# The first stage of a two-layer transformer kernel: smaller loads, another order on VectorE, later pair work and unread products on TensorE

## The reference, cut to what matters

```python
x = L0_attn_x                                   # (32, 256, 128) f32: 8192 tokens of 128
xn = _layernorm(x)
x = x + _L0_attn_ref(xn, ...) + _L0_ffn_ref(xn, ...)
# inside: gate logits = gelu(xn @ Wg1.T + bg1) ..., router = relu(xf @ Wr1 + br1) @ Wr2 + br2
xn = _layernorm(x)
x = x + _L1_attn_ref(xn, ...) + _L1_ffn_ref(xn, ...)
# _L1_attn_ref convolves with a kernel that depends on parameters alone:
#   K[h, l] = 2 Re sum_n Ct[h, n] exp(dtA[h, n] * l),  l = 0 .. 255
```

## Time and profile before

| | us |
|---|---|
| median of three runs | 1342.68 |
| profiled execution, own time | 1341.5 |
| its span | 1339.7 |
| PE's last work of the first stage ends | 91.86 |
| first load of the second stage issued by SP | 95.74 |
| first product of the second stage | 100.54 |

### The profile page before, as it was taken

How to read it: one execution, slowest core, us unless ns; L and a number is a source line. 1 busy time by engine, 2 the same in 40 slices (tenths; PEclk the granted TensorE clock), 3 DMA queues, 4 the chain that set the end, 5 groups by cost and what they waited for, 6 DMA issues and landing times. The chain is left out here.

```text
span 1339.7 us, 27122 instructions
## 1 busy us (share of the span) xinstructions
PE 1158.9 (87%) x9434; PEld 830.3 (62%) x9434; DVE 891.8 (67%) x2733; ACT 674.5 (50%) x1087; POOL 746.3 (56%) x908
## 2 busy tenths in 40 slices
PE   0771699999999997999999988999589899888884
PEld 0550355555555545899999885777456676666663
DVE  7917788888888864666666653888664588843321
ACT  1751377777777773444444333555333355533330
POOL 2300688888888862555555451333348377427776
PEclk9985699999999998999999998999699999989997
DMA  9350300000000001222222212224149022334443
GB/s 323 126 182 19 153 26 26 26 26 26 26 26 26 26 30 39 70 72 70 67 72 70 64 55 69 63 64 121 58 153 291 25 61 64 131 122 65 63 64 30
DMA packets 89568, 103.51 MB, mean 77 GB/s; under 512 B 12860, under 2 KB 75004, under 8 KB 89340
## 3 DMA queue, kind: packets, MB, share of 16 engines
q1 hardware_dynamic: 68768, 74.61, 17.6%
q0 software_dynamic: 19968, 26.63, 8.5%
q10 hardware_dynamic: 732, 0.94, 0.2%
HBM read 55.52 MB, written 46.63 MB: 76 GB/s over the span
## 5 line engine op out<-in xcount | busy, mean ns | idle before, releaser
L842 ACT ACTIVATE probs<-ps 128x1024 f32<-128x1024 f32 x256 | 255.0, 1025 | 76.5 <-PE ps L752 76.5
L1160 POOL DMA_INDIRECT y<-slot_y,where x144 | 150.9, 1048 | 144.8 <-DVE slot_y L1141 121.3
L1050 POOL DMA_INDIRECT slots<-rowbuf,slots x192 | 194.8, 1014 | 65.8 <-issue 42.8
L1221 ACT ACTIVATE slot_h<-ps,own 128x256 f32<-128x256 f32 x288 | 120.3, 470 | 153.2 <-PE ps L1192 151.5
L1192 PE MATMUL ps<-slot_x,own 128*128 128x256 f32 x576 | 140.8, 388 | 3.4 <-DVE slot_x L1130 3.1
L1204 PEld LDWEIGHTS ps<-own,slot_h 128*128 128x128 f32 x1152 | 140.0, 192 | 4.2 <-ACT slot_h L1221 0.6
L1204 PE MATMUL ps<-own,slot_h 128*128 128x128 f32 x1152 | 140.3, 276 | 0.2 <-ACT slot_h L1221 0.2
L768 PE MATMUL ps<-probs,vext 128*32 128x256 f32 x2048 | 136.9, 385 | 0.0
L1628 POOL DMA_INDIRECT out<-xT,where x64 | 99.1, 1548 | 40.6 <-DVE xT L1931 25.4
L1192 PEld LDWEIGHTS ps<-slot_x,own 128*128 128x128 f32 x576 | 105.5, 193 | 19.2 <-DVE slot_x L1130 7.5
L1779 ACT ACTIVATE h<-ps,packs 128x512 f32<-128x512 f32 x64 | 44.0, 687 | 91.2 <-PE ps L1680 89.4
(11 more groups left out here) (302 smaller groups left out, 2365.1 us busy)
## 6 DMA issues: line engine op xcount, KB each, us to landing
toeplitz<-conv_kernel SPq DMA_DIRECT2D x16, 1024.0 KB, 7.4
slots<-blank SPq DMA_DIRECT2D x26, 528.0 KB, 7.0
slot_rows<-slots SPq DMA_DIRECT2D x72, 132.0 KB, 2.2
routed<-y SPq DMA_DIRECT2D x32, 256.0 KB, 3.1
packs<-in_experts SPq DMA_DIRECT2D x1, 4624.0 KB, 14.8
packs<-in_experts SPq DMA_DIRECT2D x8, 578.0 KB, 7.2
xT<-slots SPq DMA_DIRECT2D x16, 264.0 KB, 2.7
out<-stream SPq DMA_DIRECT2D x16, 256.0 KB, 2.3
```

Source lines behind the costliest of these rows:

```text
L842: act.activation(probs[:, p % 4, :, :, :].rearrange("p j k t -> p j (k t)"), ps[:, 2 * (p % 2):2 * (p % 2) + 2, :], ACT.Exp, scale=DK ** - ...
L1050: return pool.indirect_dma_start(m["slot_dram"][layer], bass.IndirectOffsetOnAxis(ap=where, axis=0), m["rowbuf"][:, tile, :], None)
L1160: pool.indirect_dma_start(m["y_dram"][layer], bass.IndirectOffsetOnAxis(ap=where[:, j, h:h + 1], axis=0), y[:, j, h, :], None).then_inc(se ...
L1221: ins = act.activation(hidden[:, j % 2, k, :], ps[:, 2 * (j % 2) + k // 2, (k % 2) * LOT:(k % 2) * LOT + LOT], act_func, bias=own[:, j, P_ ...
```

## The change

It sets `LOADS` to 8 (8 tiles, 0.5 MB, a load) and `FIRST` to 6, orders DVE's list so that each doubling follows a measure and a normalise, and adds unread products of constants on PE: eight when the constants have landed, and four ahead of `turn(g)` for g = 1 to 5. They write bank 7, which holds nothing yet.

```diff
--- before.py
+++ after.py
@@ -204,8 +204,9 @@
     QUADS = L2 // 4
     ROUNDS = 4
     PRODUCT_BANK = (7, 5, 6, 7)
-    LOADS = 4
-    FIRST = 4
+    LOADS = 8
+    FIRST = 6
+    WARM_FIRST, WARM_EACH = 8, 4
     with ExitStack() as ctx:
         def sb(name, shape, dt=F32):
             return ctx.enter_context(nc.sbuf_tensor(name, shape, dt))
@@ -454,17 +455,13 @@
             coefficients()
             measure(0)
             begin_powers()
-            measure(1)
-            normalise(0)
-            for i in range(3):
-                double(i)
-            measure(2)
-            normalise(1)
-            double(3)
-            dve.engine_nop().then_inc(sem["pair"], 1)
-            for g in range(3, GROUPS):
+            for g in range(1, GROUPS):
                 measure(g)
                 normalise(g - 1)
+                if g <= ROUNDS:
+                    double(g - 1)
+                if g == ROUNDS:
+                    dve.engine_nop().then_inc(sem["pair"], 1)
             normalise(GROUPS - 1)
 
         @block.tensor
@@ -518,12 +515,20 @@
                                     wr2[HG:HG + R1 + 1, :], start=True, stop=True)
                 ins.then_inc(sem["logits"], 1)
 
+            def keep_warm(n):
+
+                for _ in range(n):
+                    pe.matmul(ps[:, PRODUCT_BANK[0], :], ident, cst[:, 0:4 * P], start=True, stop=True)
+
             pe.wait_ge(sem["cst_loaded"], 16)
+            keep_warm(WARM_FIRST)
             pe.wait_ge(sem["w_loaded"], 48)
             pe.wait_ge(sem["ones"], 1)
             pe.wait_ge(sem["pick"], 2)
             pe.wait_ge(sem["dcol"], 1)
             for g in range(GROUPS + 2):
+                if 1 <= g <= ROUNDS + 1:
+                    keep_warm(WARM_EACH)
                 if g < GROUPS:
                     turn(g)
                 if FIRST <= g < FIRST + 4:
```

## The result

The changed kernel took 1347.41 us (median of 20 runs, 1340.16 to 1350.68), the kernel before 1341.57 (20 runs beside them, 1334.76 to 1344.27). The ratio is 1.0040, 95% interval 1.0026 to 1.0055: slower by 5.4 us, 3.5 to 7.4. The forecast was 1349.0, slower. The profiled execution took 1348.89 us, with a span of 1347.1, 7.4 more than the one before.

A forecast was written before the change was run, and what follows sets the result against it. SP's store, blanks and barrier behind the last convolution-kernel piece were taken to end the first stage; -3.42 + 1.48 + 3.44 + 4.86 = +6.36 us on 1342.68 gave 1349.0 us, 8-in-10 range 1344.8 to 1352.6.

The forecast's parts named there:

- The chain: First stage's end: after the convolution kernel's last piece, ScalarE copies, then SP needs 17.71 us for store, blanks and barrier.
- Rival 1: First stage's end: PE's end decides instead of SP's queue, so the kernel gets faster, 1339.3 us; chance 0.06.
- rival 2: First stage's end: the shift is swallowed, time about the same, 1341.6 or 1343.3 us; chance 0.14.
- The loads: Start of the first stage: a halved first load of x lets DVE start 2.0 us earlier, bounds 0 and 2.85.
- The order on DVE: First stage: doublings behind later groups make group 4 ready at 44.12; PE gets there 3.42 us earlier, 1.42 from order.
- FIRST: PE, first stage: pair transposes and kernel pieces move behind two more groups, so the last piece comes 4.86 us later.
- The unread products: PE, first stage: early sets fit in waits; the set before group 5 is wholly on the path, 3.44 us.
- The clock: PE, first stage: the clock falls in the idle time ahead of group 4, which costs +1.48 us; bounds 0 and 2.43.
- The sum: Last piece of the convolution kernel and SP's store behind it: -3.42 + 1.48 + 3.44 + 4.86 = +6.36 us.
- the baseline: Whole kernel before the change: median 1342.68 us, profiled execution 1341.5, to which the first stage's shift is added.
- Rival 3: PE, first stage: the fills stay slow and don't lift the clock; all at half speed gives 1365 us, chance 0.03.
- Its small form: PE, first stage: only the set before group 5 is slow, +3.4 us on the forecast, 1352.5; chance 0.05.

The follow-up runs named there:

- e5: Changed kernel with SyncE's store of the convolution kernel moved behind all the blanks; ratio to the kernel before 0.9963 (0.9946 to 0.9980).
- e8: Kernel before with `FIRST` = 6, nothing else; ratio to the kernel before 1.0051 (1.0024 to 1.0079).
- e1: Changed kernel with `FIRST` back at 4; ratio to the kernel before 0.9972 (0.9955 to 0.9988).
- e2: Changed kernel without the four unread products ahead of group 5; ratio to the kernel before 1.0018 (1.0000 to 1.0036).
- e4: Changed kernel with eight unread products in place of four ahead of group 4; ratio to the kernel before 1.0027 (1.0006 to 1.0049).
- e3: Changed kernel without any unread products; ratio to the kernel before 1.0023 (1.0003 to 1.0043).
- e12: Changed kernel with `FIRST` = 4, store last, eight unread products ahead of group 4, none ahead of group 5; 1331.72 us, ratio to the kernel before 0.9931.
- e10: Changed kernel with `FIRST` = 4 and store last, without any unread product; 1332.32 us, ratio to the kernel before 0.9927.
- e13: Kernel before with the store behind all blanks and eight loads; ratio to the kernel before 0.9953 (0.9935 to 0.9971).

## Why the prediction was right

*The chain.* The step on which all hangs, that SP's chain behind the last piece ends the stage, held: 17.71 us forecast for it, 18.09 found, and e5 removed it and won 10 us. Rival 1 (PE's end decides) and rival 2 (the shift is swallowed) are out: PE ended at 94.44 (forecast 93.4), 9.1 us before the next load, and the set ahead of group 5 found no wait.

*The loads.* Forecast 2.0 us, found 2.67: DVE didn't wait at all. The rule of the Trainium skill (DMA: Bandwidth & Descriptors, the section on queues, rings and completion order) pointed nearer to 2.85, and the trace agrees with that direction; how the queues shared the engines is not shown.

*The order on DVE.* Group 4 forecast at 44.12, found at 43.36; 0.67 of the difference is the load's. The intervals between groups held to 0.1 us.

*FIRST.* Forecast +4.86 in PE's sequence. The sum above closes to 0.04 with it, and e8 shows it by itself ahead of its fall of the clock (5.12, of which 0.26 is the later start). The store of e8 and e1 has the clock's part on top.

*The unread products.* The eight first ones took 8.57 us where I allowed 13.8 (my sum for their end, 17.6, should have been 5 + 13.8 = 18.8; neither reaches the path). That the set ahead of group 5 is wholly on the path held, at 5.85 us; that it is priced at the upper level, 3.44, belongs to the clock.

*The clock.* The mechanism (idle time ahead of group 4, a low clock behind it) was right, and the size, less than half of what was measured, wrong. I let it fall ahead of group 4 and recover by the set behind it: +1.48. It fell inside group 4 and stayed low through most of the set: +0.95 and +2.41 (5.85 - 3.44), 3.36 together. I also took plain groups to raise the clock as group 2 had done in the kernel before; e2 shows two that did not.

*The sum.* +6.36 forecast for the store, +7.44 in the profiled execution: -0.76 for the earlier start and +1.88 for the clock. The timed runs gave +5.4 us, 3.5 to 7.4. So the timed number lies nearer to the forecast than the store does, and that is in part luck: the two errors have opposite signs, and the timed shift came out below the profiled one. Of the 1.6 us between 1349.0 and 1347.41, 1.1 is the baseline, 1342.68 from three runs for 1341.57 from twenty. Two things are large enough to set the profiled pair and the timed ones 2 us apart: the course of the clock, which in these profiles cost group 4 and the set behind it between 0.1 us (e4) and 3.4 (the changed kernel), and the rest of the kernel, which took 1235.1 to 1240.3. Stretches were not recorded for the timed runs, so which of the two it was is not shown.

Rival 3 (the fills don't raise the clock) is out in its full form: the sets ahead of groups 2 and 4 ran at the upper level (3.43 and 3.70 us, the one ahead of group 1 only in part, 5.07). Its small form, the set ahead of group 5 at half speed, happened in the profiled execution.

## What to carry to other kernels

Find the chain that ends a stage before pricing anything else in it: here PE is busiest, but a queue of stores behind one late result decides. Moving that store behind the transfers that don't need it took 10 us from the changed kernel, more than the 5.4 that the change had cost. Work that fills an engine's waits must be placed only where a wait is longer than the work; one set too many, in front of a group that was already ready, cost 3.5 us in e4, as much as the sets in the waits had won by holding the clock, so that e3 without products and e4 store at 82.18 and 82.19. Two equal marks can hide a gain and a loss: compare the rows between them. In the times no run shows that the products brought anything (e12 and e10). When a kernel moves by a few microseconds, compare marks in the trace (start of a store, an engine's end) along with the timed ratio, and read the clock beside both.

## What the runs showed of the hardware that I had not expected

The granted clock column shows 1.00 from the start in kernels whose first transposes take 1.1 us, for example e3 at 16.89 and 21.42; in those profiles only durations tell the level until the column first moves. PE without idle time is not the same as PE at the upper clock: in e2 two plain groups ran one behind the other at 0.50. The clock also fell where PE was busy: at 68.5 in e8 and 58.6 in e12, 0.7 and 0.2 us behind a wait of 0.91 us that left the clock up in nine other profiles, and at 88.7 in e10, 90.3 in e4 and 90.7 in e13, 0.5 to 1.4 us ahead of PE's end in the stage. In the profiles of the changed kernel (94.44 to about 95.8) and of the kernel before (91.86 to about 92.1) it fell 1.4 and 0.3 us behind PE's end. The next stage's first product, which waits for two small loads, began 4.8 us after the first one's issue where blanks were still under way (95.74 to 100.54 in the kernel before), and 3.1 us where none were (95.34 to 98.41 in e5). It is not a fixed price: in e1, where the DMA engines were busy until about 99.3, it was 3.2 us (97.89 to 101.12).
